# Another PSUM bank for the turned row maxima, and an earlier second normalization

## The reference

```python
def attention(x, ctx):                       # 16 heads of 8 columns
    q, k, v = heads(x @ Wq + bq), heads(x @ Wk + bk), heads(x @ Wv + bv)
    y = softmax(causal(q @ k.T * scale)) @ v
    qc, kc, vc = heads(x @ Wcq + bcq), heads(ctx @ Wck + bck), heads(ctx @ Wcv + bcv)
    y = y + softmax(qc @ kc.T * scale) @ vc
    return y @ Wp + bp

def ffn(x):                                  # 32 experts of 64 columns, 8 of them per token
    aff = sigmoid(x @ Wr + br)
    w = top_8(aff) / sum(top_8(aff))
    shared = (silu(x @ Wg_s + bg_s) * (x @ Wu_s + bu_s)) @ Wd_s + bd_s
    routed = sum over e of w[e] * ((silu(x @ Wg[e] + bg[e]) * (x @ Wu[e] + bu[e])) @ Wd[e] + bd[e])
    return shared + routed

x = x + attention(layernorm(x), ctx)
x = x + ffn(layernorm(x))                    # the second norm
```

## Time and profile before

| | us |
|---|---|
| median of three runs | 214.25 |
| profiled execution | 214.17 |
| its span in the trace | 212.4 |
| outside the span | 1.77 |

### The profile page before, as it was taken

One profiled execution on the slowest core, in us unless ns is written; L12 is line 12 of the kernel. 1 busy time (PEld: TensorE's weight loads), 2 busy tenths in 40 slices (PEclk: granted clock), 3 DMA queues, 4 the chain that ended last, 5 costly groups with the idle time before them and its releaser, 6 DMA issues.

```text
span 212.4 us, 4012 instructions
## 1 busy us (share of the span) xinstructions
PE 191.8 (90%) x1239; PEld 138.4 (65%) x1251; DVE 163.7 (77%) x377; ACT 141.5 (67%) x275; POOL 95.7 (45%) x149
## 2 busy tenths in 40 slices
PE   7967989999999999897998888779999999999993
PEld 2635756777667676565655555657888888887662
DVE  2889996677768876977556789896778888887882
ACT  3456778687788887786795773754577566555571
POOL 7799781242372827457444252326255332220020
PEclk9999999999999999999999999999999999999999
DMA  4265423223333242101111100000032100000003
GB/s 117 84 149 141 108 69 76 52 71 80 95 96 86 63 104 55 39 0 42 35 40 37 37 0 5 0 0 0 2 72 72 27 2 0 0 3 0 0 0 99
DMA packets 20433, 10.39 MB, mean 49 GB/s; under 512 B 11881, under 2 KB 18542, under 8 KB 20414
## 3 DMA queue, kind: packets, MB, share of 16 engines
q1 hardware_dynamic: 19290, 9.24, 17.4%
q0 software_dynamic: 672, 0.69, 1.3%
q10 hardware_dynamic: 452, 0.23, 0.5%
HBM read 4.51 MB, written 0.52 MB: 24 GB/s over the span
## 4 chain that ended last, share of the span: by engine, by line
PE 56%; DVE 14%; ACT 12%; issue 8%; POOL 7%; DMA 1%; DVEq 0%; ACTq 0%; POOLq 0%
PE psum L1282 11%; PE psum L1283 10%; PE psum L1284 10%; PE psum L1385 4%; PE psum L1472 4%; PE psum L1482 3%; ACT probs L756 3%; PE psum L1460 3%; PE psum L1613 3%; ACT query_rows L748 3%; ACT o_sb L763 2%; PE psum L1442 2%; POOL hid_lo L665 2%; PE psum L1384 1%; PE psum L1446 1%
## 5 line engine op out<-in xcount | busy, mean ns | idle before, releaser
L869 ACT ACTIVATE gate<-psum,bias_cols 128x512 f32<-128x512 f32 (+2 forms) x35 | 23.5, 674 | 29.6 <-PE psum L1284 29.5
L756 ACT ACTIVATE probs<-psum 128x512 f32<-128x512 f32 x64 | 36.5, 598 | 6.4 <-PE psum L1442 4.7
L607 POOL TENSOR_TENSOR w_ffn_lo<-w_ffn,w_ffn_hi 128x384 fp32r<-128x384 f32 x17 | 20.7, 1218 | 25.8 <-ACT w_ffn_hi L770 25.8
L1225 DVE SCALAR_TENSOR_TENSOR gated<-psum,bias_cols,gate 128x512 f32<-128x512 f32 x32 | 24.0, 749 | 10.4 <-ACT gate L869 10.4
L1282 PE MATMUL psum<-xT_hi,w_ffn_hi 128*128 128x512 f32 x66 | 26.9, 408 | 0.0
L1283 PE MATMUL psum<-xT_lo,w_ffn_hi 128*128 128x512 f32 x66 | 26.3, 398 | 0.0
L1284 PE MATMUL psum<-xT_hi,w_ffn_lo 128*128 128x512 f32 x66 | 25.9, 392 | 0.0
L1385 PE MATMUL psum<-key_blocks,query_rows 96*128 96x512 f32 x48 | 24.0, 543 | 0.3 <-issue 0.3
L1238 DVE TENSOR_TENSOR hid<-gated,psum 128x512 f32<-128x512 f32 x32 | 21.8, 683 | 1.3 <-POOL hid_lo L665 0.3
L665 POOL TENSOR_TENSOR hid_lo<-hid,hid_hi 128x512 fp32r<-128x512 f32 x9 | 11.6, 1292 | 24.0 <-ACT hid_hi L876 21.2
L631 POOL TENSOR_SCALAR_AFFINE_SELECT probs<-probs 128x512 f32<-128x512 f32 x16 | 10.4, 652 | 26.6 <-ACT probs L756 26.6
(11 more groups left out here) (179 smaller groups left out, 473.0 us busy)
## 6 DMA issues: line engine op xcount, KB each, us to landing
query_rows<-queries SPq DMA_DIRECT2D x46, 64.0 KB, 2.0
key_rows<-keys SPq DMA_DIRECT2D x39, 32.0 KB, 1.9
w_ffn<-in_L_ffn_Wg SPq DMA_DIRECT2D x16, 64.0 KB, 2.0
w_ffn<-in_L_ffn_Wu SPq DMA_DIRECT2D x16, 64.0 KB, 2.2
w_ffn<-in_L_ffn_Wd SPq DMA_DIRECT2D x16, 64.0 KB, 2.1
ckey_rows<-ckeys POOLq DMA_DIRECT2D x12, 32.0 KB, 1.9
key_rows<-keys POOLq DMA_DIRECT2D x9, 32.0 KB, 1.8
x_sb<-in_x SPq DMA_DIRECT2D x2, 128.0 KB, 2.8
```

Of the source, the lines that this page charges most:

```text
L607: ins = pool.tensor_tensor(w_ffn_lo[:, k, :, :], w_ffn[:, k, :, :], w_ffn_hi[:, k, :, :].bitcast(F32), ALU.subtract).then_inc(ffn_lo, 1)
L756: act.activation(probs[:, i % 2, c, :], bank(B_ST + c % 2), ACT.Exp, scale=SCALE).then_inc(exp_done, 1)
L869: act.activation(gate[rows_of(n), n % 3, part], psum[of, B_GATE + n % 2, part], ACT.Silu, bias=bias_cols[of, BIAS_GATE + u:BIAS_GATE + u + ...
L1225: dve.scalar_tensor_tensor(out=gated[:, n % 3, :], in0=bank(B_UP + n % 2), scalar=bias_cols[:, BIAS_UP + u:BIAS_UP + u + 1], in1=gate[:, n ...
```

## The change

- The turned maxima go to bank 3 (`B_MAX`), the second bank of tile 1, in place of bank 7. `turn_max` takes `B_MISC` no more; in its place the last matmuls of tile 1, the next writers of bank 3, wait for ScalarE's copy of the maxima that were turned just before.
- The two idle matmuls stay before `turn_max(0)` and `turn_max(1)`; before `turn_max(2)` they go to bank 6 behind a wait for the context values, and before `turn_max(3)` they are gone.
- `long_part("norm", b)` for b = 0 and 1 stands ahead of tile 0's maxima.
- GpSimd, once it has the reciprocal root, waits until VectorE has applied it.

```diff
+B_MAX = B_NAT1 + 1
@@ GpSimd, tail(name, b)
                     pool.tensor_tensor(rstd[:, 2 * b:2 * b + 2], var_eps[:, 2 * b:2 * b + 2], minus_half[:, 0:2],
                                        ALU.pow).then_inc(have_rstd, 1)
+                    pool.wait_ge(x2_normed, 2 * b + 2)
@@ ScalarE, shift(i)
-                         psum[0:GROUP, B_MISC, :].rearrange("p (s n) -> p s n", s=2)).then_inc(shift_placed, 1)
+                         psum[0:GROUP, B_MAX, :].rearrange("p (s n) -> p s n", s=2)).then_inc(shift_placed, 1)
@@ VectorE, maxima(i, outputs)
+                for name, b in between_at.get(i - 2, ()):
+                    long_part(name, b)
                 dve.wait_ge(m_nat, 3 * i + 1)
                 tile_0()
...
                 context()
-                for name, b in between_at.get(i - 2, ()):
-                    long_part(name, b)
                 if outputs >= 0:
                     normalize(outputs)
@@ TensorE, natural(i, output), tile_1()
                     masked(bank(B_NAT1), 1, 0)
-                    masked(bank(B_NAT1 + 1), 1, 1).then_inc(m_nat, 1)
+                    if i:
+                        pe.wait_ge(shift_placed, i)
+                    masked(bank(B_MAX), 1, 1).then_inc(m_nat, 1)
@@ TensorE, turn_max(i)
-                take_misc(shift_placed, i + 1)
-                if i < 4:
+                if i < 2:
                     run_idle(2, B_MISC)
+                if i == 2:
+                    pe.wait_ge(have_cvalue, 2)
+                    run_idle(2, B_OUT)
                 pe.wait_ge(max_done, 3 * i + 3)
                 for n in range(4):
-                    ins = pe.matmul(psum[0:GROUP, B_MISC, P * n:P * (n + 1)], row_max[:, i % 2, n, :],
+                    ins = pe.matmul(psum[0:GROUP, B_MAX, P * n:P * (n + 1)], row_max[:, i % 2, n, :],
                                     ident_r[:, :], start=True, stop=True)
```

## The result

The changed kernel ran at 209.44 us (median of four runs), the kernel before beside it at 214.24 us; the ratio of the times is 0.9734, with an interval of 0.9705 to 0.9764, so 2.4 to 3.0% faster. Predicted were 208.4 us, 206.9 to 210.2.

The account below looks back on a forecast made before the run. TensorE, 90% busy and at its upper clock, was taken as the engine to watch; gains of 2.7 + 0.3 + 1.27 + 0.25 + 0.9 + 0.45 = 5.87 us from 214.17 gave 208.30, 208.4 on the median's scale, range 206.9 to 210.2.

Parts of the forecast that it names:

- the rival of 209.3: Feed-forward stage: delayed hid_lo or a new collision keeps TensorE waiting elsewhere, the 0.9 us is lost; 13%.
- my 5.87: Whole kernel: summed gain in us, 2.7 + 0.3 + 1.27 + 0.25 + 0.9 + 0.45.
- The bank, 2.7 us: Attention steps: turned outputs no longer wait for ScalarE's copy of the turned maxima; 3.1 less 0.4 for step 10.
- Step 10, counted as 0: Step 10: closing its 0.4 us hole only lengthens the 0.61 wait for VectorE's normalized outputs, to near 1.0.
- The clock, 3%: Steps 1 to 3: with idle matmuls gone TensorE might fall to 1.2 GHz, costing up to 5 us a step; 3%.
- a slice with a clock under 9: Changed profile: a slice with the granted clock below 9 would be a sign that the prediction was wrong.
- The norm of batch 1, 1.27: Step 12: moving the norm ahead of tile 0 removes TensorE's whole 1.27 us stall before x2_turn.
- The norm of batch 0, 0.25: Step 8: the same move removes the 0.25 us stall between last scores and x2_turn, taken whole.
- The norm of batch 3, 0.9: Feed-forward item 3: with GpSimd waiting the norm takes 0.68 instead of 1.54 us, 0.9 less on TensorE's path.
- The idle matmuls, 0.45: Step 2: removing the idle pair cuts first scores to tile 0 from 1.27 to 0.82 us; nothing in step 1.
- The collision at item 5: Batch 3's routing: expected unchanged; rival, VectorE's L1135 starts before GpSimd's hid_lo, gaining 1.1 us, 207.3; 20%.
- The holes: Attention steps: ScalarE's chain sets the step, half or more of the 2.7 us returns as waits, around 210.4; 14%.

Follow-up runs that it names:

- e11: Changed kernel with two idle matmuls added in step 10 and two instead of five at the very start: median 207.99 us, ratio 0.9701 to the kernel before.
- e8: Kernel before without the pair of idle matmuls ahead of turn_max(3), nothing else: median 214.12 us, ratio 0.9970 to the kernel before.
- e1: Changed kernel run again unchanged, for a further profile: median 209.62 us, ratio 0.9718 to the kernel before.
- e10: Changed kernel without the norm's move and GpSimd's wait, plus five idle matmuls in step 10: median 211.09 us, ratio 0.9862 to the kernel before.
- e4: Changed kernel without GpSimd's wait for VectorE to apply the root: median 210.07 us, ratio 0.9757 to the kernel before.
- e9: e6 with GpSimd's hid_lo of item 4 held back until batch 3's routing weights are made: median 207.15 us, ratio 0.9662 to the kernel before.
- e6: Changed kernel with five idle matmuls ahead of step 10's tail: median 208.03 us, ratio 0.9697 to the kernel before.

## Why the prediction was right, and where it was not

It can be held against the steps one by one; without that, 209.44 would have pointed at the rival of 209.3, which did not happen. Start of a step is its first scores' first matmul (L1437, L1443); lengths in us, of the kernel before and of e11, which has the changed order and kept its clock:

| step | 2 | 3 | 4 | 5 | 6 | 7 | 8 | 9 | 10 | 11 | 12 | 13 | 14 |
|---|---|---|---|---|---|---|---|---|---|---|---|---|---|
| before | 6.44 | 5.93 | 6.20 | 5.23 | 5.44 | 5.85 | 5.75 | 5.80 | 6.41 | 6.03 | 6.86 | 5.79 | 4.33 |
| e11 | 5.88 | 5.62 | 5.89 | 4.77 | 5.08 | 5.53 | 5.26 | 5.49 | 6.87 | 5.73 | 5.05 | 5.49 | 3.94 |

The sums differ by 5.46 us; with 0.94 at item 3 that is 6.4, against 6.3 between the times at full clock and my 5.87. So 208.1 is what the sum should be held against, and it came within 0.3 us of that partly by luck: the terms below miss in both directions.

- **The bank, 2.7 us.** Mechanism right, size too small: the nine steps that only the bank touches (3 to 7, 9, 11, 13, 14) gave 0.30 to 0.46 each, 3.1 together, where I had counted 0.27 or so a step. I took the idle time of the waits view for the whole of what a wait costs; it leaves out that a matmul may start ahead of its forerunner's modelled end (step 6: an idle time of 0.27, a gain of 0.42).
- **Step 10, counted as 0.** Here the forecast failed. I wrote that its wait would be "near 1.0". It was 1.66, and even at full clock the step is 0.46 longer than before. Of the 1.05 that the wait grew, 0.59 is TensorE's: it starts its last scores 3.06 us into the step (80.94) where it was 3.65 (84.47). I had counted 0.4 for that. The rest is VectorE's: it gets from `exp_neg` to the end of the normalized outputs in 4.22 us, where it took 3.77 (81.71 to 85.48), and 0.44 of this is `key_blocks`, 1.05 us where it took 0.61 (80.25, before 83.18). GpSimd's selection now comes right behind its mask work (rows below), while before there was a gap of 0.16 between them into which VectorE's two instructions went, and the selection took 0.83 in place of 0.64. So the two met in both kernels, and it is now VectorE that waits. Counted from the first scores, VectorE's `exp_neg` (0.89), its `key_blocks` (2.37, before 2.36) and the selection (2.63) stand where they stood; the masks stand 0.17 later (1.16, before 0.99) and fill the gap. That this is why the step is longer is read from the rows; no run kept the two apart.

```profile
79.04 1.48 POOL L597 TENSOR_SCALAR_AFFINE_SELECT spread_f<-spread_f 128x512 f32<-128x512 f32 x2
80.51 0.64 POOL L633 TENSOR_SCALAR_AFFINE_SELECT probs<-probs 128x512 f32<-128x512 f32 x1
```

- **The clock, 3%.** I looked for it where idle matmuls went, in steps 1 to 3, and e8 shows nothing there. It came where two holes became one, at a price of 1.5 us, in six of nine runs of the changed kernel by their times and mean clocks (one of the six has a profile, e1). The prediction had named a slice with a clock under 9 as a sign of being wrong, and that sign came. It had also taken the upper level in one trace for what every run has; the kernel before falls too, in 14 of 39 runs. The fall in step 10, and not the sum, is the distance from 208.1 to the measured 209.44, and the reason that a kernel whose gain I had under-estimated came out slower than forecast.
- **The norm of batch 1, 1.27.** Right: `x2_turn` 0.33 behind the scores; with 0.30 for the maxima's wait and the closed hole, step 12 is 1.81 shorter (e10, the bank alone, has 0.53 of it).
- **The norm of batch 0, 0.25.** Not so: VectorE waited 0.42 for the root, which I had given no time, and tile 0 came right behind the norm, so `x2_turn` is still 0.51 behind its scores (70.19, 70.70). The norm had taken only 0.76 in this step (the row under e4), so there was little to win by its length. But without the norm's part the bank gains nothing in step 8 (5.82 in e10), with it 0.49.
- **The norm of batch 3, 0.9.** 0.94, as worked out.
- **The idle matmuls, 0.45.** Too large. It is 0.82 from scores to tile 0 in step 2 (34.34, 35.16), as worked out, but a gain there is not kept to the step's end: alone it gives 0.25 (e8), and with the bank step 2 is 0.56 shorter. In step 1 TensorE waits 1.06 for GpSimd's key blocks instead of 0.16, and nothing is gained, as said.
- **The rivals.** The collision at item 5 was decided as before (e1), and e9 shows what it would have given. The feed-forward gain was not eaten: 0.94 at item 3. The holes did not return: no step but 10 is longer.

## What to carry to other kernels

Closing many small waits moves all work on one engine against the work that did not move: look in each step where the two now meet, and add up the holes that become one. When the times of a kernel fall into two groups, compare the granted clock of single stretches first; two idle matmuls in the right place gave 1.5 us here, more than GpSimd's wait did. Look at more than one profile of the kernel before as well: a fall that one trace does not show can be in a third of the runs. Where a VectorE instruction is several times as long in one place as in another, see whether it ends with a GpSimd instruction; if it does, holding GpSimd back for it is cheap when GpSimd's reader is far off.

## What the runs showed of the hardware that I had not expected

- Behind a single hole of 1.66 us, in a kernel that is 92% busy, the granted clock was 0.50 for 3.4 us in the profile of e1, and six of nine runs have its time. In e8 it was 0.50 for 3.4 us, from 1.9 us after a hole of 1.39. The same hole at item 3 of the kernel before, its holes of 0.41 and 0.61 with 2.0 us of work between them, and one of 1.22 behind two idle matmuls (e11) showed none in the profiles taken. What decides between a hole with a fall and one without is not shown. The Trainium skill ("TensorE: Matmul & The Clock Gate", section "What's actually happening") says that activity is what releases the throttle; e6 and e11 agree, as idle matmuls in the hole kept the clock up.
- The same pair of VectorE instructions took 0.60 us beside a resting GpSimd or its memset, 0.76 beside its masks and 1.28 to 1.60 beside its two-input instructions.
- One execution of 302.2 us went with a granted clock near 0.56 from 6 us on, with no other of its kind in over 100 runs of these kernels.
